# Summing over key blocks: one DVE reduction pair per head pair, or a tree of additions on POOL with two product buffers

## The reference, cut to what matters

```python
scores = einsum('bhsd,bhjkd->bhsjk', q, kb) * SCALE      # j: key block, k: key in it
scores = where(diag_mask, -inf, scores)                  # later keys of the own block
w = softmax(scores, axis=-1)                             # within each block
w = w * include                                          # blocks up to the query's own
out = einsum('bhsjk,bhjkd->bhsd', w, vb)
out = out / (sum(w) + 1e-6)
```

## Time and profile before

| | us |
|---|---|
| median of 3 runs | 517.65 |
| the runs | 516.83, 517.65, 522.6 |
| profiled execution, first to last instruction | 518.4 |

### The profile page before, as it was taken

How to read it: one execution, slowest core, us unless ns; L and a number is a source line. 1 busy time by engine, 2 the same in 40 slices (tenths; PEclk the granted TensorE clock), 3 DMA queues, 4 the chain that set the end, 5 groups by cost and what they waited for, 6 DMA issues and landing times.

```text
span 518.4 us, 10886 instructions
## 1 busy us (share of the span) xinstructions
PE 430.6 (83%) x3616; PEld 397.7 (77%) x3616; DVE 333.3 (64%) x936; ACT 180.5 (35%) x409; POOL 165.1 (32%) x272
## 2 busy tenths in 40 slices
PE   1747399799949996999658997899959999898885
PEld 1635379688849985999658896899959999797785
DVE  4526379848838884688524885498728878757241
ACT  2521025514414342532433224433424244433140
POOL 4420500002614152315421154233523124317162
PEclk9875559968969997999978999799979999999898
DMA  8599843912870079004920039201960110010000
GB/s 168 164 104 173 71 153 78 105 34 82 122 92 3 0 153 108 18 1 122 109 49 3 1 121 105 51 2 43 143 70 1 42 32 3 2 32 10 22 1 22
DMA packets 44083, 33.89 MB, mean 65 GB/s; under 512 B 2980, under 2 KB 41892, under 8 KB 43836
## 3 DMA queue, kind: packets, MB, share of 16 engines
q1 hardware_dynamic: 44028, 33.18, 40.2%
HBM read 23.21 MB, written 9.96 MB: 64 GB/s over the span
## 4 chain that ended last, share of the span: by engine, by line
PE 58%; DMA 19%; SPq 7%; DVE 6%; issue 5%; POOL 3%; ACT 2%; POOLq 0%; DVEq 0%; ACTq 0%
PE X L776 28%; DMA KS<-parts_d 16%; PE PO L870 11%; SPq L420 7%; PE SA L831 3%; PE SB L854 3%; DMA parts_d<-parts 2%; PE X L799 2%; DMA x_sb<-x 2%; PE SA L834 1%; PE SA L832 1%; PE SA L833 1%; PE SB L857 1%; PE SB L856 1%; PE SB L855 1%
## 5 line engine op out<-in xcount | busy, mean ns | idle before, releaser
L665 DVE TENSOR_REDUCE nmax<-SA 128x12 f32<-128x384 f32 x128 | 66.7, 554 | 74.7 <-PE SA L834 71.6
L870 PE MATMUL PO<-VB,PT 128*128 128x68 f32 x768 | 98.9, 280 | 0.0
L870 PEld LDWEIGHTS PO<-VB,PT 128*128 128x128 f32 x768 | 93.9, 197 | 3.1 <-issue 2.8
L598 POOL TENSOR_TENSOR hid<-gsil,ups 128x256 f32<-128x256 f32 x64 | 47.3, 742 | 125.8 <-DVE ups L760 123.8
L831 PE MATMUL SA<-KS,QS 96*128 96x256 bf16 x128 | 42.2, 330 | 48.9 <-DMA KS<-parts_d 47.4
L776 PE MATMUL X<-x_h,wgu_h 128*128 128x256 f32 x256 | 78.3, 306 | 0.6 <-ACT sbc L513 0.5
L776 PE MATMUL X<-x_l,wgu_h 128*128 128x256 f32 x256 | 73.5, 287 | 0.0
L776 PE MATMUL X<-x_h,wgu_l 128*128 128x256 f32 x256 | 73.2, 286 | 0.0
L492 ACT ACTIVATE PT<-SB 128x384 f32<-128x384 f32 x128 | 56.1, 489 | 47.1 <-PE SB L857 36.6
L604 POOL TENSOR_TENSOR hid_l<-hid,hid_h 128x256 fp32r<-128x256 f32 x64 | 46.4, 733 | 39.1 <-ACT hid_h L524 38.8
L831 PEld LDWEIGHTS SA<-KS,QS 96*128 96x128 bf16 x128 | 14.0, 109 | 56.8 <-issue 28.8
(11 more groups left out here) (118 smaller groups left out, 1002.7 us busy)
## 6 DMA issues: line engine op xcount, KB each, us to landing
parts_d<-parts SPq DMA_DIRECT2D x16, 384.0 KB, 2.8
QS<-parts_d SPq DMA_DIRECT2D x48, 128.0 KB, 7.3
KS<-parts_d SPq DMA_DIRECT2D x48, 128.0 KB, 7.9
x_sb<-x SPq DMA_DIRECT2D x8, 256.0 KB, 10.7
raw<-wgu SPq DMA_DIRECT2D x8, 256.0 KB, 3.6
xres<-x SPq DMA_DIRECT2D x8, 256.0 KB, 2.7
out<-x SPq DMA_DIRECT2D x16, 128.0 KB, 1.8
max_d<-mt_sb SPq DMA_DIRECT2D x8, 192.0 KB, 10.5
```

Of the source, the lines that this page charges most:

```text
L598: nc.gpsimd.tensor_tensor(hid[k % 2][:, :], gsil[k % 2][:, :], ups[k % 2][:, :], ALU.mult)\
L665: nc.vector.tensor_reduce(nmax[:, 0:NC_, h], SA[h % 2][:, 0:SC] .rearrange("p (c s) -> p c s", s=BS), AX.X, ALU.max, negate=True)\
L870: last = pe.matmul(o[:, dst:dst + PW], PT[k % 2][:, n, src:src + P], v[:, t, 2 * k + n, :], start=True, stop=True)
```

## The change

The sums over the key blocks are taken from DVE. DVE's stage o is a reciprocal straight from PSUM and one product for both heads, into one of two buffers `oblk`. A new stage rd on POOL adds the blocks up in four additions, through a tile `fold`, and writes `o_sb`. rd.k waits for the product of pair k; the product of pair k waits for rd.(k-2). oT waits for all eight rd. The 64 rd stages are written into POOL's list; the other lists keep their order. In place of the added 1, `VB` holds 1e-30 where it held zero in the summing column, by one more memset for each of its two buffers; the excluded blocks' sums are no longer zero. PV writes its groups in another order (first the first query tile's), so that the product can take both heads in one access pattern. DVE's gate result goes into th itself, so the tanh of expert k waits for hid of expert k-2, where it waited for the reading of the bank; `beats` is written over `above`.

```diff
 POOL_ORDER = (
-    "ln0 z0 ln1 qP0 kP0 ln2 qP1 kP1 ms0 qP2 ln3 kP2 ms1 res0 qP3 top0 kP3 hp0.0-1 ms2 hl0.0-1 hp0.2-3 "
-    "hl0.2-3 hp0.4 hl0.4 hp0.5-6 hl0.5 hp0.7 hl0.6-7 res1",
-
-    "ln4 top1 qP4 kP4 hp1.0 ms3 hp1.1 hl1.0 hp1.2 hl1.1 hp1.3 hl1.2 hp1.4 hl1.3 hp1.5 hl1.4 hp1.6 hl1.5 "
-    "hp1.7 hl1.6-7 res2",
-
-    "top5 ms7 hp5.0-1 hl5.0-1 hp5.2-3 res6 hl5.2 hp5.4 hl5.3 hp5.5 hl5.4 hp5.6 top6 hl5.5-6 hp5.7 hl5.7 "
-    "hp6.0-1 hl6.0 hp6.2 hl6.1-2 hp6.3-4 hl6.3 res7 hp6.5 hl6.4-5 hp6.6-7 hl6.6-7 top7 hp7.0-1 hl7.0-1 "
+    "ln0 z0 ln1 qP0 kP0 ln2 qP1 kP1 ms0 qP2 ln3 kP2 ms1 rd0.0-7 rd1.0 res0 rd1.1-2 qP3 top0 kP3 rd1.3 hp0.0-1 ms2 "
+    "hl0.0-1 hp0.2 rd1.4 hp0.3 hl0.2 rd1.5-6 hl0.3 hp0.4 hl0.4 hp0.5 rd1.7 hp0.6 hl0.5 hp0.7 hl0.6 rd2.0 hl0.7 res1",
+
+    "ln4 rd2.1-2 top1 qP4 rd2.3 kP4 rd2.4 hp1.0 ms3 hp1.1 hl1.0 rd2.5 hp1.2 rd2.6 hl1.1 hp1.3 rd2.7 hl1.2 hp1.4 "
+    "hl1.3 hp1.5 hl1.4 hp1.6 hl1.5 rd3.0 hp1.7 hl1.6-7 res2",
+
+    "rd6.1-2 top5 ms7 rd6.3-4 hp5.0 rd6.5-6 hp5.1 hl5.0 rd6.7 hl5.1 hp5.2-3 rd7.0 res6 hl5.2 hp5.4 hl5.3 hp5.5 "
+    "hl5.4 hp5.6 rd7.1 hl5.5 hp5.7 rd7.2 top6 hl5.6-7 rd7.3-4 hp6.0-1 hl6.0 rd7.5 hp6.2 rd7.6-7 hl6.1-2 hp6.3-4 "
+    "hl6.3 res7 hp6.5 hl6.4-5 hp6.6-7 hl6.6-7 top7 hp7.0-1 hl7.0-1 "
...
+    oblk = [sb(f"oblk{n}", [P, 2, NC_, HD], F32) for n in range(2)]
+    fold = sb("fold", [P, 2, 2 * BPT, HD], F32)
...
 # ACT, stage th
-    act.wait_ge(drained["gu"], b.times(NE, k - 1))
+    act.wait_ge(hid_done, b.times(NE, k - 1))
...
 # POOL, stage z
+    nc.gpsimd.memset(sums[:, :, HD], FLOOR).then_inc(v_cleared, 1)
...
+    if stage == "rd":
+        pool.wait_ge(pv_drained, b.times(8, k + 1))
+        if k == 0:
+            wait(pool, ready["oT"], b.times(1))
+            stand_alone(pool)
+        wait(pool, o_done, b.times(8, k))
+        ob = oblk[k % 2]
+        nc.gpsimd.tensor_tensor(fold[:, :, BPT:2 * BPT, :], ob[:, :, BPT:2 * BPT, :], ob[:, :, 2 * BPT:NC_, :],
+                                ALU.add).then_inc(fold_done, 1)
+        nc.gpsimd.tensor_tensor(fold[:, :, 0:2, :], ob[:, :, 0:2, :], ob[:, :, 2:BPT, :], ALU.add)\
+            .then_inc(fold_done, 1)
+        pool.wait_ge(fold_done, b.times(24, 3 * k + 2))
+        nc.gpsimd.tensor_tensor(fold[:, :, BPT:BPT + 2, :], fold[:, :, BPT:BPT + 2, :],
+                                fold[:, :, BPT + 2:2 * BPT, :], ALU.add).then_inc(fold_done, 1)
+        pool.wait_ge(fold_done, b.times(24, 3 * k + 3))
+        pairs = fold[:, :, :, :].rearrange("p h (t c) d -> p t h c d", t=TT)
+        nc.gpsimd.tensor_tensor(o_sb[:, :, 2 * HD * k:2 * HD * (k + 1)].rearrange("p t (h d) -> p t h d", h=2),
+                                pairs[:, :, :, 0, :], pairs[:, :, :, 1, :], ALU.add).then_inc(o_done, 1)
...
 # DVE, stage o
     dve.wait_ge(pv_ready, b.times(8, k + 1))
-    wait(dve, inv_done, b.times(8, k))
-    nc.vector.tensor_tensor(lsum[:, :, :], po[:, :, :, HD],
-                            excluded.unsqueeze(1).to_broadcast([P, 2, NC_]), ALU.add).then_inc(sum_done, 1)
-    dve.wait_ge(sum_done, b.times(8, k + 1))
     wait(dve, pv_drained, b.times(8, k))
-    nc.vector.reciprocal(linv[:, :, :], lsum[:, :, :]).then_inc(inv_done, 1)
+    nc.vector.reciprocal(linv[:, :, :], po[:, :, :, HD]).then_inc(inv_done, 1)
     dve.wait_ge(inv_done, b.times(8, k + 1))
-    for h in range(2):
-        last = nc.vector.tensor_tensor(oblk[:, h, :, :], po[:, h, :, 0:HD],
-                                linv[:, h, :].unsqueeze(2).to_broadcast([P, NC_, HD]), ALU.mult)
-    last.then_inc(pv_drained, 1)
...
-    for t, c in ((0, slice(NBLK, NC_)), (1, slice(0, NBLK))):
-        nc.vector.tensor_reduce(o_sb[:, t, ...], oblk[:, :, c, :], AX.X, ALU.add)
+    if not (b.trip is None and b.base == 0 and k < 2):
+        dve.wait_ge(o_done, b.times(8, k - 1))
+    parted = PO[k % 2][:, 0:2 * NC_ * VW].rearrange("p (c v) -> p c v", v=VW)
+    nc.vector.tensor_tensor(oblk[k % 2][:, :, :, :].rearrange("p h c d -> p (h c) d"), parted[:, :, 0:HD],
+                            linv[:, :, :].rearrange("p h c -> p (h c)").unsqueeze(2)
+                            .to_broadcast([P, 2 * NC_, HD]), ALU.mult).then_inc(pv_drained, 1)
...
 # DVE, stage gd
-    nc.vector.scalar_tensor_tensor(out=gsil[k % 2][:, :], in0=th[k % 2][:, :], scalar=1.0,
+    nc.vector.scalar_tensor_tensor(out=th[k % 2][:, :], in0=th[k % 2][:, :], scalar=1.0,
...
 # PE, stage PV
-    for dst, src, t in ((0, P, 0), (PW, S, 1), (2 * PW, 0, 0)):
+    for dst, src, t in ((PW, P, 0), (2 * PW, S, 1), (0, 0, 0)):
```

More of the change, by code:

```diff
@@ L44 @@
 MASKED = -1.0e30
+FLOOR = 1.0e-30
 Q_PART = [0, 1, 2, 0, 1, 0]
@@ L235, in preln_block_attention_moe @@
         ident_f = cst[:, 0:P]
-        excluded = cst[:, P:P + NC_]
         norm = cst[:, P + NC_:P + NC_ + TT]
@@ L263, in preln_block_attention_moe @@
         PT = [sb(f"PT{n}", [P, 2, SC], F32) for n in range(2)]
-        lsum = sb("lsum", [P, 2, NC_], F32)
         linv = sb("linv", [P, 2, NC_], F32)
-        oblk = sb("oblk", [P, 2, NC_, HD], F32)
+        oblk = [sb(f"oblk{n}", [P, 2, NC_, HD], F32) for n in range(2)]
+        fold = sb("fold", [P, 2, 2 * BPT, HD], F32)
         o_sb = sb("o_sb", [P, TT, H], F32)
@@ L280, in preln_block_attention_moe @@
         equal = sb("equal", [P, TT, NE, NE], F32)
-        beats = sb("beats", [P, TT, NE, NE], F32)
         rank = sb("rank", [P, TT, NE], F32)
@@ L291, in preln_block_attention_moe @@
         th = [sb(f"th{n}", [P, S], F32) for n in range(2)]
-        gsil = [sb(f"gsil{n}", [P, S], F32) for n in range(2)]
         ups = [sb(f"ups{n}", [P, S], F32) for n in range(2)]
@@ L326, in preln_block_attention_moe @@
         pv_ready, pv_drained = sem("pv_ready"), sem("pv_drained")
-        sum_done, inv_done, o_done = sem("sum_done"), sem("inv_done"), sem("o_done")
+        inv_done, fold_done, o_done = sem("inv_done"), sem("fold_done"), sem("o_done")
         lmax_done, ldiff_done, lexp_done = sem("lmax_done"), sem("ldiff_done"), sem("lexp_done")
@@ L471, in _ @@
                     if b.trip is None and b.base < 2:
-                        act.wait_ge(v_cleared, (BPT + 1) * (b.base + 1))
+                        act.wait_ge(v_cleared, (BPT + 2) * (b.base + 1))
                     else:
@@ L536, in _ @@
                         if n:
-                            pool.wait_ge(v_cleared, n * (BPT + 1))
+                            pool.wait_ge(v_cleared, n * (BPT + 2))
                         nc.gpsimd.memset(VB[n][:, :, :, :], 0.0).then_inc(v_cleared, 1)
+                        pool.wait_ge(v_cleared, n * (BPT + 2) + 1)
+                        sums = VB[n][:, :, :, :].rearrange("p t h (j v) -> p (t h j) v", v=VW)
+                        nc.gpsimd.memset(sums[:, :, HD], FLOOR).then_inc(v_cleared, 1)
                         for j in range(BPT):
-                            pool.wait_ge(v_cleared, n * (BPT + 1) + 1 + j)
+                            pool.wait_ge(v_cleared, n * (BPT + 2) + 2 + j)
                             nc.gpsimd.memset(VB[n][BS * j:BS * (j + 1), :, :, VW * j + HD:VW * (j + 1)], 1.0)\
                                 .then_inc(v_cleared, 1)
-                    pool.wait_ge(v_cleared, 2 * (BPT + 1))
+                    pool.wait_ge(v_cleared, 2 * (BPT + 2))
                 if stage in ("ln", "res"):
@@ L597, in _ @@
                         pool.wait_ge(hid_lo, b.times(NE, k - 1))
-                    nc.gpsimd.tensor_tensor(hid[k % 2][:, :], gsil[k % 2][:, :], ups[k % 2][:, :], ALU.mult)\
+                    nc.gpsimd.tensor_tensor(hid[k % 2][:, :], th[k % 2][:, :], ups[k % 2][:, :], ALU.mult)\
                         .then_inc(hid_done, 1)
@@ L670, in _ @@
                     dve.wait_ge(pv_ready, b.times(8, k + 1))
-                    wait(dve, inv_done, b.times(8, k))
-                    nc.vector.tensor_tensor(lsum[:, :, :], po[:, :, :, HD],
-                                            excluded.unsqueeze(1).to_broadcast([P, 2, NC_]), ALU.add)\
-                        .then_inc(sum_done, 1)
-                    dve.wait_ge(sum_done, b.times(8, k + 1))
                     wait(dve, pv_drained, b.times(8, k))
-                    nc.vector.reciprocal(linv[:, :, :], lsum[:, :, :]).then_inc(inv_done, 1)
+                    nc.vector.reciprocal(linv[:, :, :], po[:, :, :, HD]).then_inc(inv_done, 1)
                     dve.wait_ge(inv_done, b.times(8, k + 1))
-                    wait(dve, o_done, b.times(16, 2 * k))
-                    for h in range(2):
-                        last = nc.vector.tensor_tensor(oblk[:, h, :, :], po[:, h, :, 0:HD],
-                                                linv[:, h, :].unsqueeze(2).to_broadcast([P, NC_, HD]), ALU.mult)
-                    last.then_inc(pv_drained, 1)
-                    dve.wait_ge(pv_drained, b.times(8, k + 1))
-                    if k == 0:
-                        wait(dve, ready["oT"], b.times(1))
-                    for t, c in ((0, slice(NBLK, NC_)), (1, slice(0, NBLK))):
-                        nc.vector.tensor_reduce(
```

(13 more changed lines are left out.)

## The result

The changed kernel takes 532.27 us (531.39 to 533.83, four runs) where the kernel before takes 517.47, beside it on the same chip: a ratio of 1.0253, interval 1.0206 to 1.03. That is slower by 14.8 us. The forecast was 528.4 in 520 to 537, slower with 0.80.

The account below looks back on a forecast made before the run. A loop step was taken as PE's work plus DMA, with DVE covered. 2.8 + 7.2 + 1.7 - 1.0 = +10.7 on the 518.4 us span gave 529.1, less 0.75 to the median of the runs: 528.4, range 520 to 537.

Parts of the forecast that it names:

- The price of a tree: POOL's four additions per pair of heads with waits on its own results: 1.65 us, bounds 0.9 and 3.0.
- r: The forecast's time for one pair's four additions on POOL, waits on its own results included: 1.65 us.
- Place A: Drain, POOL's list before top6: rd7.1 and rd7.2 delay the router parts, so PE's sT6 stands 2.8 us more.
- Place B: Drain, before oT7: rd7.5 to rd7.7 queue behind the late hl6.0 on POOL, so PE stalls 7.2 us.
- The clock behind B: After PE's stall before oT7 the granted clock drops as at the turn of the loop: 1.7 us lost.
- The loop at nothing: Loop steps: rd2.3 between qP4 and kP4 makes kP 0.5 us late, hidden by 0.8 us of cover; counted 0.
- oT6's own wait: Drain: the sums reach oT6 0.4 us late; x2S6 behind it on DVE comes earlier by as much.
- the loss there was paid before: +0: Clock after sT6 in the drain: already 0.79 before the change, so no added loss, at most +1.7 us.
- The turn, -1.0: Turn of the loop: PE waited 1.28 us for xn behind a DVE o unit; its shortening gives 1.0 back.
- Rival 1: Not slower: later PE idle time in the drain pays back some 9 us of the stalls, 519.4 us; chance 0.13.
- Rival 2: Small strided additions on POOL cost like 256 elements, 3.0 us per pair: +23.5, 541 us; chance 0.08 including what lies between.
- Rival 3: Additions on POOL hold up DVE's small two-input router operations of top6: +1.7, 530.1 us; chance 0.04.

Follow-up runs that it names:

- both places mended: Changed kernel with rd7.5-7 put ahead of hl6.0, rd7.1-2 ahead of hl5.4 and top6 right behind hp5.6 in POOL's list: 520.92 us, ratio 1.004.

## Why the forecast was right, and where it was not

**Right, with sizes.** That DVE's saving is worth nothing: the kernel with all edits but the trees, 13.5 us of DVE lighter, shows it at 1.0001, and the loop's waits are 48.8 and 49.2 with and without the trees. The price of a tree: 1.53 for 1.65, or 1.67 where the next one follows. (In busy time DVE came to 267 for 255 and POOL to 253 for 270: the sum of means counts overlaps twice, and r holds waits.) Place A: the wait grew from 1.05 to 3.51, +2.5 for +2.8. Place B: 6.75 for 7.2; with r at 1.53 the forecast's own sum gives 6.8. The clock behind B: 2.0 for 1.7 (2.2 to 2.3 from oT7 to x2T7, with 0.2 of it the wait before x2T7). The loop at nothing: the first table is 0.3 ahead at oT6, and the KS waits are 47.5 to 50.2 in the seven profiles with trees, 47.4 and 49.2 in the two of before. oT6's own wait and the x2S6 behind it moved against each other as said (0.2 to 0.6 for the one, 2.0 to 1.7 for x_l).

**The step that failed: "so the loss there was paid before: +0".** It was read from one row, 0.79 over the 8 us from 448, as if the kernel before always lost clock behind its wait of 1.05 us. It does not. Six profiles have that short wait: 0.79 follows it in two of them (one is the kernel before, one has both places mended and kP4 moved), 1.00 in four. With the wait of 3.51 it was 0.57 to 0.60 in all four:

```profile
449.00:457.00 8.00, 7.93 (x42) 6.77 (x42) 0.20 (x1) 2.61 (x8) 0.73 (x1) 0.57 0.01 2
477.25:482.25 5.00, 5.00 (x24) 5.00 (x25) 1.45 (x3) 1.99 (x5) 2.11 (x4) 0.50 0.00 0
```

These are the changed kernel's rows behind A and behind B. From sT6 to oT7, without the wait at B, PE needed 21.05 to 21.4 us behind a wait of 3.5 and 18.17 to 18.4 where the clock stayed at 1.00. That is +2.7 to +3.3, and +3.2 for the changed kernel against the second profile of before; the forecast's upper end, taken from the turn of the loop, was 1.7. Only against the profile that the forecast used, which took 19.7 at 0.79, is it 1.7.

**The second error, which hid the first.** The sum was set on a span of 518.4, and the text took 0.75 off, the distance to the median of time. But the time of a run lies above its own span, by some 1.8 us (531.39 for 529.6, 517.36 for 515.5), so a span of 518.4 would belong to a run of some 520. That profile was a longer one than is usual: the next one had 515.5 with the same waits. +10.7 on 518.4 gives 529.1, +14.3 on 515.5 gives 529.8. The match of the spans is thus luck; as an effect, 10.7 was 3.6 us short of the spans' 14.3 and 4.1 short of the medians' 14.8.

**The turn, -1.0, was wrong.** PE's wait for xn there is 1.14 for 1.28, so 0.1 came. Before, the gate followed the unit on DVE at once; now it waits 1.00 us for ScalarE's tanh, which itself waits for PE. Before and after (second number us, last idle before):

```profile
280.29 0.42 DVE L758 SCALAR_TENSOR_TENSOR gsil<-th,X 128x256 f32<-128x256 f32 x1
```

```profile
277.92 0.42 DVE L766 SCALAR_TENSOR_TENSOR th<-th,X 128x256 f32<-128x256 f32 x1 [1.00 <-ACT th L519]
```

Counted from the oT at the turn (273.51 and 271.24), the gate starts 6.78 us behind it before and 6.68 after.

The forecast took the time of the unit ahead as the reason for the wait, without asking what else the DVE work behind it needs.

**The rivals.** Rival 1, stalls paid back by later idle time: the first table has +14.15 at x2T7 and +14.26 at dn7, so nothing came back. Rival 2, a dear tree: the additions with pieces of 16 elements cost what their elements say. Rival 3, contention at the router: it is there, but small and hidden. From logit to score DVE took 4.38 to 4.40 us in the four profiles with rd7.1 and rd7.2 ahead of top6, and 4.00 to 4.03 in the six others. Score ended at 445.48, before POOL's turn, so the 0.4 cost nothing.

**The sum by the runs:** -0.5 + 2.5 + 3.2 + 6.7 + 2.2 = +14.1, against 14.3 between the two spans.

**What stays open.** The kernels with both places mended are some 0.4% above the kernel before, at the edge of their intervals. No wait of PE behind oT6 is longer in them; the 2 us are the slow clock behind x2T7. Why it holds longer there in the four kernels that mend B, wholly or in part, and not in the others, is not shown: the kernel with the sums on DVE, whose POOL list is that of before, took 1.3 us more there in its one profile and still ran at 1.0001. It may be chance in single profiles. Why the loop takes up to 6 us more in one profile than in another is open as well. No version here beats the kernel before.

## What to carry to other kernels

Moving work to an engine that is half idle is safe only where nothing ahead of it in that engine's list waits for something later than the moved work's own operands: at both places POOL had idle time enough, and the trees stood behind instructions that were late or ahead of one that was urgent. Price a stall of PE in a dense stream with the clock behind it, 2 to 3 us here for each, and read that clock from more than one profile before calling it paid. And where 66 us of an engine's work go and it waited for others anyway, look first at whom the freed engine would have released; here it was nobody.

## What the runs showed of the chip

- Behind a wait of PE of 3.5 us the granted clock was 0.57 to 0.60 over the next 8 us (four profiles), behind 6.7 us 0.50 over the next 5 us (three profiles), behind 5.47 us 0.63. Behind 1.05 us it was 1.00 in four profiles and 0.79 in two. Since a fraction of 0.50 of 2.4 GHz is its lower level of 1.2 GHz, the first 5 us behind B ran wholly at that one. The cost was not in proportion to the wait: behind the shorter one 2.7 to 3.3 us were lost, behind the longer one some 2.0.
- An addition on POOL costs by its elements even in strided pieces, where nothing holds it up: 0.22 us for 16 elements, 0.323 to 0.327 for 64, 0.466 for 128, 0.73 for 256.
- POOL and DVE held each other up where DVE had two inputs in SBUF. A tree addition that began 0.10 us behind such a subtraction took 0.77 us, where the median of its line is 0.32:

```profile
122.31 0.68 DVE L632 TENSOR_TENSOR wdn_l<-raw,wdn_h 128x512 fp32r<-128x512 f32 x1
...
122.41 0.77 POOL L606 TENSOR_TENSOR fold<-fold 128x64 f32<-128x64 f32 x1
```

  Another, at 138.19, took 0.90 for 0.45. On DVE's side it is the 0.4 us of the router above. The product of 384 elements, with one input in PSUM, took 0.556 to 0.560 in all 64. The Trainium skill (GPSIMD Engine Reference, Specifications) names this contention on the SBUF interfaces that GpSimd shares with VectorE, for DVE instructions with two SBUF inputs; the rows agree. The means hide it, since few additions are hit.
- A reciprocal of 24 elements took 0.303 us from PSUM, as from SBUF, so an addition made only to bring sums out of PSUM buys nothing there.
